# Graph network kernel on one Trainium2 core: carry between runs by feature chunk, and a rearranged head

## The reference, cut to what matters

```python
def _sage_conv(x, src, dst, Wl, bl, Wr):
    agg = jax.ops.segment_max(x[src], dst, num_segments=x.shape[0])
    agg = jnp.where(jnp.isfinite(agg), agg, 0.0)
    return agg @ Wl + bl + x @ Wr

h = jnp.maximum(_layernorm(x, axis=-1), 0.0)
h = leaky_relu(_sage_conv(h, src, dst, Wl1, bl1, Wr1), 0.01)   # 128 -> 256
h = leaky_relu(_sage_conv(h, src, dst, Wl2, bl2, Wr2), 0.01)   # 256 -> 256
h = leaky_relu(_sage_conv(h, src, dst, Wl3, bl3, Wr3), 0.01)   # 256 -> 128
out = x + h
```

## Time and profile before

| | before |
|---|---|
| median of 3 runs | 6193.24 us |
| the profiled execution's own time | 6178.24 us |
| its span, first to last instruction | 6176.4 us |
| busy share POOL / DVE / PE / ACT | 75% / 47% / 11% / 4% |
| mean DMA rate | 176 GB/s |

### The profile page before, as it was taken

How to read it: one execution, slowest core, us unless ns; L and a number is a source line. 1 busy time by engine, 2 the same in 40 slices (tenths; PEclk the granted TensorE clock), 3 DMA queues, 4 the chain that set the end, 5 groups by cost and what they waited for, 6 DMA issues and landing times. The chain is left out here.

```text
span 6176.4 us, 24426 instructions
## 1 busy us (share of the span) xinstructions
PE 695.5 (11%) x2214; PEld 399.1 (6%) x2214; DVE 2882.1 (47%) x3614; ACT 227.9 (4%) x664; POOL 4607.9 (75%) x4878
## 2 busy tenths in 40 slices
PE   0111111111100780000000000057000000000003
PEld 0000000000000340000000000034000000000002
DVE  4333333333333555555555555565555555555556
ACT  1000000000000110000000000011000000000001
POOL 6777777777777677777777777767777777777776
PEclk8555555555555655555555555565555555555556
DMA  4333333333333576666666666667666666666665
GB/s 129 107 107 108 105 107 107 107 107 107 107 104 107 171 236 210 209 210 209 210 211 210 211 209 210 209 205 246 210 210 210 210 211 208 212 208 210 209 210 171
DMA packets 435669, 1088.94 MB, mean 176 GB/s; under 512 B 101413, under 2 KB 154154, under 8 KB 435642
## 3 DMA queue, kind: packets, MB, share of 16 engines
q0 software_dynamic: 206976, 530.17, 30.4%
q1 hardware_dynamic: 203706, 537.55, 23.4%
q10 hardware_dynamic: 24960, 20.95, 1.1%
HBM read 555.13 MB, written 533.14 MB: 176 GB/s over the span
## 5 line engine op out<-in xcount | busy, mean ns | idle before, releaser
L365 POOL DMA_INDIRECT ring<-features,stage x4692 | 4439.4, 946 | 1451.3 <-issue 1406.8
L656 DVE TENSOR_TENSOR ring<-banks,ring 128x1024 f32<-128x1024 f32 (+1 forms) x1173 | 1226.5, 1046 | 3066.8 <-DMA ring<-features,stage 3049.3
L635 DVE TENSOR_TENSOR banks<-ring,banks 128x1024 f32<-128x1024 f32 (+1 forms) x1173 | 1232.2, 1050 | 37.6
L869 PE MATMUL banks<-ident,ring 128*128 128x128 f32 x20 | 5.0, 428 | 3763.5 <-DVEq L668 3763.5
L843 PE MATMUL banks<-dst_low,own 128*128 128x394 bf16 x200 | 99.5, 498 | 1459.8 <-DVE own L619 1459.8
L869 PEld LDWEIGHTS banks<-ident,ring 128*128 128x128 f32 x20 | 3.9, 222 | 3764.9 <-DVEq L668 3538.1
L827 PE MATMUL banks<-wr,h_turned 128*128 128x256 f32 (+1 forms) x490 | 204.0, 559 | 95.9 <-ACT h_turned L965 95.9
L1009 ACT ACTIVATE agg<-zeros 128x512 f32<-128x512 f32 x75 | 47.3, 630 | 3957.4 <-PE banks L901 3957.4
L390 POOL DMA_INDIRECT ring<-running_max_log,end_row x147 | 141.6, 964 | 60.5 <-issue 43.9
L624 DVE COPY stage<-edges 128x8 int32 (+1 forms) x588 | 129.1, 220 | 84.8 <-DVE banks L635 25.8
L829 PE MATMUL banks<-b,ones 1*128 1x256 f32 (+1 forms) x294 | 141.9, 579 | 0.0
(11 more groups left out here) (104 smaller groups left out, 560.8 us busy)
## 6 DMA issues: line engine op xcount, KB each, us to landing
running_max_log<-ring SPq DMA_DIRECT2D x782, 512.0 KB, 3.2
running_max_log<-ring SPq DMA_DIRECT2D x391, 256.0 KB, 2.3
ring<-features,stage POOLq DMA_INDIRECT x4692, 2.8
h_in<-features ACTq DMA_DIRECT2D x98, 128.0 KB
features<-h_out SPq DMA_DIRECT2D x48, 256.0 KB, 2.2
ring<-x SPq DMA_DIRECT2D x5, 640.0 KB, 10.4
features<-ring SPq DMA_DIRECT2D x5, 640.0 KB, 3.7
h_in<-features ACTq DMA_DIRECT2D x49, 64.0 KB
```

Of the source, the lines that this page charges most:

```text
L365: pool.indirect_dma_start(ring[:, c * w:(c + 1) * w], None, tables[l], bass.IndirectOffsetOnAxis(ap=stage[:, b, u:u + 1].bitcast(U32), axi ...
L635: dve.tensor_tensor(sum_ps[:, 0:CHAINS * w].rearrange("p (h f) -> p h f", h=CHAINS), group(g - 1).rearrange("p (h f) -> p h f", h=CHAINS), ...
L656: dve.tensor_tensor(group(g), sum_ps[:, 0:CHAINS * w], group(g), ALU.max).then_inc(turn, 1)
```

## The change

Two parts. **Join by chunk:** PE signals after each chunk's transposes of 128 features, DVE scans a chunk as soon as that chunk is there, PE turns it back into a PSUM bank of its own, and the patch maximum is taken chunk by chunk, each over 4 x 128 elements; SP's patch store waits for both. **Head:** x comes in five parts of 6, 11, 12, 12 and 8 tiles (49 tiles; the 50th was padding and is no longer loaded, normalised or stored). `dst` is one flat array in DRAM with a word ahead and a word behind, and one DMA on SP's queue brings each run with both of its neighbours (393 words), issued after the third part of x; `src` follows on the same queue. The 8 loads of single words go. Weights are issued after the stores of the first table. ACT loads its table with a dummy square root at the start, and square roots and reciprocals are placed within a part's work. In the last part DVE normalises 3 tiles itself. The order check moves behind all statistics: one subtraction with a running maximum over 4 x 391 (kept in `falls`), one small comparison. `stage` is filled straight from `src` before the branch, and the gathers are opened by a semaphore increment after the branch, ahead of the reordering of `src`. The restart values come from `falls` in one instruction instead of two.

```diff
+CHUNKS = (6, 11, 12, 12, 8)
+ACT_TILES = (4, 8, 9, 8, 3)
+POOL_TILES = (2, 3, 3, 4, 2)
+VARS_AFTER = (4, 8, 6, 3)
+RECIPROCAL_AFTER = 4
...
+    dst_seen = bass.AP(dst.tensor, 0, [[RUN, P], [P * RUN, CHAINS], [1, RUN + 2]])
...
+                for k in range(CHUNKS[s]):
+                    if s and k == RECIPROCAL_AFTER:
+                        normalise(s - 1)
+                    dve.bn_stats(stats[:, k, :], x_all[:, FROM[s] + k, :]).then_inc(stats_done, 1)
...
-            def check_order():
-
-                dve.wait_ge(order_loaded, (LOADS - 1) * DMA)
-                dve.tensor_tensor(scratch_runs[:, :, 1:RUN], dst_runs[:, :, 1:RUN], dst_runs[:, :, 0:RUN - 1],
-                                  ALU.is_lt).then_inc(order_checked, 1)
...
+            rest = slice(FROM[HEAD_STEPS - 1] + ACT_TILES[-1] + POOL_TILES[-1], END_TILES)
+            dve.wait_ge(norm_ready, 2 * HEAD_STEPS)
+            for k in range(rest.start, rest.stop):
+                dve.tensor_scalar(h0_all[:, k, :], x_all[:, k, :], rstd[:, k:k + 1], shift[:, k:k + 1],
+                                  ALU.mult, ALU.add).then_inc(h0_last_scaled, 1)
+            dve.wait_ge(h0_last_scaled, rest.stop - rest.start)
+            dve.tensor_scalar(h0_all[:, rest, :], h0_all[:, rest, :], 0.0, None, ALU.max).then_inc(h0_last_done, 1)
+
+            dve.wait_ge(dst_loaded, DMA)
+            dve.tensor_tensor_reduce(out=falls, in0=dst_w[:, :, 0:RUN], in1=dst_runs, scale=1.0, scalar=0.0,
+                                     op0=ALU.subtract, op1=ALU.max, accum_out=highest_fall[:, :]
+                                     ).then_inc(order_checked, 1)
+            dve.wait_ge(order_checked, 1)
+            dve.tensor_scalar(disorder[:, :], highest_fall[:, :], 0.0, None, ALU.is_gt).then_inc(order_checked, 1)
+
+            def stage_first():
+
+                dve.tensor_copy(stage[:, 0:BLOCKS - 1, :].rearrange("p b (j h) -> p (b j) h", h=CHAINS),
+                                src_runs.rearrange("p (h j) -> p j h", h=CHAINS)[:, 0:(BLOCKS - 1) * BLOCK_GROUPS, :]
+                                ).then_inc(first_staged, 1)
+
+            dve.wait_ge(src_loaded, DMA)
+            stage_first()
...
+            dve.wait_ge(first_staged, 1)
+            dve.sem_inc(block_scanned, BLOCKS - 1)
             dve.tensor_copy(src_turns, src_runs.rearrange("p (h j) -> p h j", h=CHAINS)).then_inc(prep_done, 1)
-            dve.wait_ge(prep_done, 1)
-            dve.tensor_copy(stage[:, 0:BLOCKS - 1, :],
...
-            dve.tensor_tensor(restart_turns[:, :, 1:RUN], dst_runs[:, :, 1:RUN], dst_runs[:, :, 0:RUN - 1],
-                              ALU.not_equal).then_inc(prep_done, 1)
+            dve.tensor_scalar(restart_turns[:, :, 1:RUN], falls[:, :, 1:RUN], 0.0, LOWEST,
+                              ALU.not_equal, ALU.mult).then_inc(prep_done, 1)
...
-                dve.wait_ge(carry_turned, l + 1)
                 dve.wait_ge(pass_diag, CHAINS + 1)
                 for c in range(kc):
+                    dve.wait_ge(carry_turned, CHUNKS_TO[l] + c + 1)
                     dve.tensor_tensor_scan(carry_scan[:, c, 1:RUNS + 1], pass_row[:, :],
                                            carry_ps[:, c * RUNS:(c + 1) * RUNS], 0.0,
                                            ALU.add, ALU.max).then_inc(carried_on, 1)
-                dve.wait_ge(incoming_turned, l + 1)
                 dve.wait_ge(patch_landed, DMA * CHAINS * (l + 1))
-                dve.tensor_tensor(patch[:, 0:CHAINS * w], patch[:, 0:CHAINS * w], back_ps[:, 0:CHAINS * w],
-                                  ALU.max).then_inc(patched, 1)
+                patch_rows = patch[:, 0:CHAINS * w].rearrange("p (h f) -> p h f", h=CHAINS)
+                for c in range(kc):
+                    dve.wait_ge(incoming_turned, CHUNKS_TO[l] + c + 1)
+                    dve.tensor_tensor(patch_rows[:, :, c * P:(c + 1) * P], patch_rows[:, :, c * P:(c + 1) * P],
+                                      back_ps[:, c * RUNS:(c + 1) * RUNS].rearrange("p (h f) -> p h f", h=CHAINS),
+                                      ALU.max).then_inc(patched, 1)
...
-                        turn = pe.transpose(back_ps[:, h * w + c * P:h * w + (c + 1) * P],
+                        turn = pe.transpose(back_ps[:, c * RUNS + h * P:c * RUNS + (h + 1) * P],
                                             carry_scan[:, c, h * P:(h + 1) * P], ident[:, :])
-                turn.then_inc(incoming_turned, 1)
+                    turn.then_inc(incoming_turned, 1)
...
+            act.wait_ge(const_done, 1)
+            nc.scalar.activation(warm[:, :], eps[:, :], ACT.Sqrt).then_inc(act_ready, 1)
...
+            for s in range(3):
+                load_x(s)
+            sp.dma_start(dst_w, dst_seen).then_inc(dst_loaded, DMA)
+            for s in range(3, HEAD_STEPS):
+                load_x(s)
+            sp.dma_start(src_runs.rearrange("p (h j) -> p h j", h=CHAINS),
+                         src.rearrange("(h p) j -> p h j", p=P)).then_inc(src_loaded, DMA)
```

More of the change, by code:

```diff
@@ L39, in gnn_program @@
     RUN = src.shape[1]
+    edge_dst = dst[1:1 + src.shape[0] * RUN].rearrange("(r j) -> r j", j=RUN)
+    dst_seen = bass.AP(dst.tensor, 0, [[RUN, P], [P * RUN, CHAINS], [1, RUN + 2]])
     COLS = CHAINS * RUN
@@ L43, in gnn_program @@
     LAST = COLS - (STEPS - 1) * RING_COLS
-    TAIL_STEPS = TILES // TAIL_TILES
+    HEAD_STEPS = len(CHUNKS)
+    FROM = [sum(CHUNKS[:s]) for s in range(HEAD_STEPS + 1)]
     PAIRS = TILES // 2
@@ L234, in gnn_program @@
         LAYERS = len(shapes)
-        LOADS = 2 + 2 * CHAINS
-        CONSTS = 16 + 2 * CHAINS
-        PREP = 21 + 2 * CHAINS
+        LOADS = 6
+        CONSTS = 14 + 2 * CHAINS
+        PREP = 20 + 2 * CHAINS
         ENDS = 11
         N_WEIGHTS = 3 * LAYERS * DMA
+        CHUNKS_TO = [sum(k for k, _ in shapes[:l]) // P for l in range(LAYERS + 1)]
         PER_OUT = PAIRS // STORES * DMA
@@ L250, in run_neighbours @@
         def run_neighbours(runs):
[L252 to L257, removed]
+            own_runs = runs.rearrange("(h p) j -> p h j", p=P)
+            pairs = [(prev_last[1:P, :], own_runs[0:P - 1, :, RUN - 1]),
+                     (prev_last[0:1, 1:CHAINS], own_runs[P - 1:P, 0:CHAINS - 1, RUN - 1]),
+                     (next_first[0:P - 1, :], own_runs[1:P, :, 0]),
+                     (next_first[P - 1:P, 0:CHAINS - 1], own_runs[0:1, 1:CHAINS, 0])]
             return pairs
@@ L917, in _ @@
         def _(act):
[L918 to L924 removed]
             def deviation(s):
[L928 to L929 removed]
+                t = slice(FROM[s], FROM[s + 1])
+                act.wait_ge(var_done, FROM[s + 1])
                 nc.scalar.activation(std[:, t], mean_var[:, t, 1], ACT.Sqrt, bias=eps[:, 0:1]).then_inc(std_done, 1)
[L933 to L941 removed]
+            act.wait_ge(const_done, 1)
+            nc.scalar.activation(warm[:, :], eps[:, :], ACT.Sqrt).then_inc(act_ready, 1)
+            act.wait_ge(act_ready, 1)
+            deviation(0)
+            for s in range(HEAD_STEPS):
+                act.wait_ge(norm_ready, 2 * (s + 1))
+                for k in range(ACT_TILES[s]):
+                    if s < HEAD_STEPS - 1 and k == VARS_AFTER[s]:
+                        deviation(s + 1)
+                    t = FROM[s] + k
+                    nc.scalar.activation(h0_all[:, t, :], x_all[:, t, :], ACT.Relu, bias=shift[:, t:t + 1],
+                                         scale=rstd[:, t:t + 1]).then_inc(h0_done, 1)
+                if s < HEAD_STEPS - 1 and VARS_AFTER[s] == ACT_TILES[s]:
+                    deviation(s + 1)
+            act.wait_ge(const_done, CONSTS)
             act.sem_inc(upto_counted, 1)
@@ L950, in _ @@
                 if l == 0:
[L951 removed]
+                    act.wait_ge(h0_stored, DMA * HEAD_STEPS)
                 else:
@@ L1072 @@
     edges = inputs["src"].shape[0]
-    group = P * TAIL_TILES
-    rows = -(-nodes // group) * group
+    rows = -(-nodes // (2 * P)) * 2 * P
     runs = CHAINS * P
@@ L1088 @@
         "src": filled(np.asarray(inputs["src"]), runs * run, 0),
-        "dst": filled(np.asarray(inputs["dst"]), runs * run, NO_NODE),
+        "dst": np.concatenate([[-1], filled(np.asarray(inputs["dst"]), runs * run, NO_NODE).ravel(), [1 << 24]]
+                              ).astype(np.int32),
     }
```

140 lines of the change are left out of this document (57 added, 83 removed).

## The result

| | before | after |
|---|---|---|
| median, us | 6193.18 (6192.24 to 6194.87, 9 runs) | 6176.97 (6174.81 to 6179.77, 9 runs) |
| ratio, 95% interval | 1 | 0.9974 [0.9965, 0.9983] |
| profiled execution, own time | 6178.24 | 6179.77 |
| first gather starts, us | 46.03 | 32.73 |
| tenth gather starts, us | 60.81 | 46.26 |

The account below looks back on a forecast made before the run. POOL's 4692 gathers at 1.25 us bound the kernel, 5865 us untouched. Earlier first gather 16.5, less preparation 1.2 and joins 0.2, gives 15.1 us: median 6193.2 to 6178 us, range 6171 to 6186.

Parts of the forecast that it names:

- The first gather: End of the head: first gather moves from 46.0 to 29.5 us, a gain of 16.5 us (13.5 to 18.5).
- path 2: Head, DVE's order check and branch: `unsorted` known near 24.8 us, next work of DVE and POOL at 27.1.
- Path 1: Head, computing by DVE, ACT and POOL: last store landed at 27.0 us if the queue is free.
- Path 3: Head, all loads and stores in order through SP's queue: 26.8 us without a gap, ending at 28.8.
- slower case: Head, SP's queue at the 251 GB/s seen beside single-word loads: first gather at 32.5 us.
- The preparation: DVE's preparation beside the first gathers: 6.2 us of instructions cost them 4.7 us, 1.2 more than before.
- 75%: First gathers: share of the length of DVE's instructions beside them that they lose, from 3.33 of 4.44 us before.
- The joins: Joins of layers 2 and 3: patch maximum in two instructions, 0.1 us worse each, 0.2 in all; cover 3.8 us.
- rival 1: Head: preparation blocks gathers in full and the queue is slow; 6179.6 us, with both 6182.6; chance 0.25.
- Rival 4: Head: DVE's idle time becomes a wait for `dst` or `src`; up to 5 us less gain, 6183; chance 0.02.
- Rival 2: Head: stores and loads overlap, gathers slip between DVE's instructions; first gather at 27.5, time 6173 us; chance 0.15.
- Rival 3: All 4692 gathers: their distance rises, 3.2 ns each eats the gain, from 5.9 ns slower (6205.7 us); chance 0.03.

Follow-up runs that it names:

- a_head_only: The kernel after with the new head kept and the chunked join undone; 6986.95 us, ratio 0.9974 to the kernel before on the same chip.
- c_warm: The kernel after plus one extra, waited-for indirect DMA on POOL right after its iota; 6984.8 us, ratio 0.997 to the kernel before.
- b_check_late: The kernel after with DVE's order check held until POOL has finished its last tiles; 6993.66 us, ratio 0.9977 to the kernel before.
- b_before_sems: The kernel before with four unused semaphores allocated ahead of the gathers' ones; 7006.14 us, ratio 0.9997 to the kernel before.

## Why the prediction was right, and where it was off

**The head as the source of the gain: right.** a_head_only has all of it. DVE's 7.99 us of idle time in its statistics are down to 1.45 and they start at 4.40, for 4.5.

**The first gather: 32.7, not 29.5.** Two steps failed. In path 2, the branch, `unsorted` was known at 26.97 instead of 24.8, and the sum gave POOL the price of DVE, 2.34 us from the copy to the next work. DVE paid less, 28.82 - 26.97 = 1.85 us; POOL paid 32.73 - 26.97 = 5.76. Before, 5.7 us also lay between POOL's load of `unsorted` (40.3) and the first gather (46.03), but there they ended with the store's landing, and any price of POOL's own was under that cover. When the cover went, the 2 us between landing (30.8) and gather appeared. c_warm shows that an earlier indirect DMA takes them away.

**Path 1 was off by 3.5 us.** The last store was issued at 27.3, and the sum has it 3.7 - 0.5 ahead of 27.0, at 23.8. The shift of the fourth part was ready at 20.31, for 18.7: 1.6 us later. The wait of 1.45 us for the second part of x, which the sum doesn't have, is about as long. And POOL's two last tiles cost 2.63 us, for 0.88, beside the two-input check; b_check_late gives them 1.00. The prediction weighed DVE against the gathers, never against POOL's own tiles. With the branch free, the landing at 30.8 alone would have put the first gather near 31.0 (the 0.26 us of c_warm behind it), so 1.5 of the 3.2 us are path 1's and 1.7 path 2's. **Path 3, the queue, was not the bound:** it was taken at 284 GB/s, and the stretches of 2 us in which stores and loads mix show 347 to 365 (last column). The packets of 4 bytes beside the 251 GB/s of the earlier trace rows, on which its slower case rests, were also about a thousand (8 loads of 128 words), not thousands:

```profile
16.00:18.00 2.00, 0.00 (x0) 0.00 (x0) 1.97 (x11) 1.50 (x5) 1.32 (x3) 1.00 1.07 365
18.00:20.00 2.00, 0.00 (x0) 0.00 (x0) 1.86 (x18) 1.93 (x6) 1.17 (x1) 1.00 1.14 347
```

So the gain at the first gather was 13.3 us, not 16.5: just under the lower end of 13.5 given for it.

**The preparation: 2.3 us lost, not 4.7.** The excess is 2.38 - 0.95 = 1.43 us and 1.78 - 0.95 = 0.83. It cost 1.2 us less than before, where 1.2 more were forecast. For the instructions that did lie beside gathers 75% came out near enough, though it is no fixed share, as b_check_late shows: the first gather, at 32.73, lay beside the rest of L568 and L578, and the long one at 39.17 beside L592. But the gathers started 3.2 us later than forecast, behind L557, L558 and L563, and the four comparisons (L582, 1.44 us from 35.11), counted with 75%, cost the gather beside them nothing (0.95). The two errors, 3.2 us lost and 2.4 saved, have opposite signs: the net of head and preparation is 14.55 us, for 15.3. They hang together in part, since a later first gather leaves more of the preparation behind it; that they come so near to each other is luck.

**The joins: right.** Two maxima of 0.64 us, and 0.1 us more a layer. The cover, 3.8 us before, is 4.7 now (6102.44 - 6097.78, where PE's transposes end), and nothing used it.

**Sum.** 14.55 - 0.2 = 14.35 us, for 15.1, inside the interval of the measured 16.2.

**The prediction's own signs.** Most of the signs on the head failed: it called itself wrong if the first gather came later than 32 us, and it came at 32.73; the copy of `unsorted` came at 26.97, for 25; the last store landed 2 us ahead of the gather, not just ahead; the gathers' excess was 2.3 us, for 3 to 6; and the distance was 1.2527 us, for 1.25. So the gain and its source were right, and the time was hit by a sum of which two terms were off. The choice to take the gain from the median and not from the profiled execution was right too, but without a reason in the rows: for the profiled execution the same sum was 16.7 us off.

**The rivals.** Of rival 1 the slow queue didn't occur; gathers were held to an instruction's end, but cost 2.3 us and not the 6.2 of all the instructions. Rival 4 (new waits for `dst`) didn't occur. Rival 2's overlap of stores and loads did, but the branch hid it. Rival 3's mechanism occurred: 2.7 ns a gather, under the 5.9 from which it decides, though its chance had been put at 0.03 with the argument that no instruction in the loop is edited. b_before_sems shows that this argument doesn't hold. What it cost in the timed runs of the result stays open: the profiles put 12.7 us on it, while the timed medians lie 16.2 us apart, and no profile shows where a run of the kernel before spends 6193 us. If the before that was timed had the 1.2500 us of its profile, the gain should have been near zero; so its timed runs differ from its profile in something unseen.

Not tried: holding DVE's preparation back until the first gathers are through.

## What to carry to other kernels

A price hidden under a wait isn't in the row that names the wait. When an edit takes the cover away, look for the work of the same engine beneath it, above all a first use, and bound it on its own. When two engines are brought closer together in time, list what each runs beside the other on both sides, not only beside the critical operation. Where one instruction repeats thousands of times, compare its median before and after, to the nanosecond, before crediting a gain to an edit.

## What the runs showed of the hardware that was not expected

- POOL's first indirect DMA starts 5.5 us after the branch's load (27.2 and 32.73); when one has been issued at 1.83 us, the first gather starts 3.9 us after the load, 0.26 us behind the store's landing.
- A DVE instruction with two SBUF inputs (1.77 us) more than doubles the time of two POOL tensor_scalar tiles, 2.63 against 1.00 us.
- A gather beside which a DVE instruction of 0.98 us from SBUF to SBUF starts ends 0.12 us behind it (b_check_late, 34.91 and 36.34), and one that starts while L592, 1.54 us, runs ends 0.7 us behind it (after, 40.95).
- DVE's instructions with an operand in PSUM take 1.8 instead of 0.98 us and leave the gathers alone (0.94 to 1.15 us); L592, 1.54 us between SBUF and SBUF, makes one 1.8 to 2.1 us long.
- The median gather is 946, 949, 957 or 960 ns by program on the three chips of the experiments (947 for after in the result), the same again when a program was run again, and four unused semaphores are enough to change it.
- The same kernel takes 6193 us in the result and 7005 to 7010 on the three chips of the experiments, with the median gather the same 946 ns.
